# Graph network kernel: node blocks ordered by edge count, and a relational layer's block work placed at fixed steps of its edge loop

## The reference, cut to what matters

```python
def _rgcn_layer(x, src, dst, edge_type, edge_attr, W, root, bias, nn_w, nn_b):
    edge_w = edge_attr @ nn_w.T + nn_b            # (E, 256) from 32 attributes
    msg = relu(x[src] * edge_w)
    out = x @ root + bias
    for r in range(3):                            # relations
        mask = edge_type == r
        s = segment_sum(where(mask, msg, 0), dst)
        cnt = segment_sum(mask, dst)
        out = out + (s / max(cnt, 1)) @ W[r]
    return out
...
h = x
for l in range(3): h = _rgcn_layer(h, ...)
x = layernorm(x + h)
```

## Time and profile before

| what | value |
|---|---|
| time, median of 3 runs | 4121.45 us (4115.07 to 4121.66) |
| span of the profiled execution | 4117.9 us (the page gives no other time for it) |
| busy: PE, DVE, ACT, POOL | 3104.7, 2876.4, 1533.8, 2706.7 us |
| instructions | 112272 |
| granted TensorE clock, mean | 0.894 |

### The profile page before, as it was taken

The page is one execution under the profiler, slowest core; times in us unless marked ns, Lnnn a source line. Parts: engine busy times, 40 slices in busy tenths (PEclk is TensorE's granted clock), DMA queues, the critical chain, the costliest instruction groups (busy, mean ns, idle before and its releaser), DMA issues.

```text
span 4117.9 us, 112272 instructions
## 1 busy us (share of the span) xinstructions
PE 3104.7 (75%) x28301; PEld 2331.3 (57%) x28301; DVE 2876.4 (70%) x10466; ACT 1533.8 (37%) x4045; POOL 2706.7 (66%) x2886
## 2 busy tenths in 40 slices
PE   6886027777776987777648888897888888888887
PEld 4443015555554565555436666676666667666666
DVE  9998026777776677777667777766777766777777
ACT  1000006777764267777623333212333321333320
POOL 5777747777774377777647777636777745777760
PEclk8777558999998999999969999899999989999988
DMA  3222157888884578888834444314443323444430
GB/s 77 55 57 48 27 162 218 237 237 236 237 230 84 162 228 238 237 237 236 200 108 124 123 120 120 108 58 125 122 120 115 114 73 90 122 119 117 116 105 32
DMA packets 386267, 574.01 MB, mean 139 GB/s; under 512 B 134783, under 2 KB 272433, under 8 KB 386163
## 3 DMA queue, kind: packets, MB, share of 16 engines
q0 software_dynamic: 155264, 442.19, 37.8%
q1 hardware_dynamic: 176106, 123.76, 10.1%
q10 hardware_dynamic: 54794, 6.81, 1.1%
HBM read 531.37 MB, written 41.08 MB: 139 GB/s over the span
## 4 chain that ended last, share of the span: by engine, by line
PE 19%; issue 19%; DVE 16%; DVEq 10%; DMA 10%; POOL 7%; ACT 2%; ACTq 1%; POOLq 0%; SPq 0%
DMA ht<-kv_rows,gidx 6%; PE bank L1210 6%; DVE region L1873 6%; DVEq L728 4%; PE bank L1049 3%; POOL ht L584 3%; PE bank L1197 3%; DVE rings L1854 3%; DMA gring<-kv_rows,gidx 2%; DVE rings L1860 2%; POOL gring L618 2%; PE bank L1124 2%; POOL gring L584 2%; PE bank L1145 2%; PE bank L1157 1%
## 5 line engine op out<-in xcount | busy, mean ns | idle before, releaser
L618 POOL DMA_INDIRECT gring<-h_rows,gidx x1248 | 1201.1, 962 | 464.3 <-issue 317.2
L1210 PE MATMUL bank<-rings 128*128 128x96 f32 x6168 | 914.8, 297 | 247.2 <-DVE region L1873 245.3
L1210 PEld LDWEIGHTS bank<-rings 128*128 128x128 f32 x6168 | 811.0, 205 | 444.8 <-DVE region L1873 406.8
L1281 ACT ACTIVATE rings<-rings 128x512 f32<-128x512 f32 x771 | 485.6, 630 | 1366.2 <-DVE rings L1854 1313.0
L1854 DVE TENSOR_TENSOR rings<-bank,gring 128x256 f32<-128x256 f32 x1542 | 582.4, 420 | 390.1 <-PE bank L1210 195.2
L584 POOL DMA_INDIRECT gring<-kv_rows,gidx x512 | 485.7, 949 | 245.9 <-issue 133.4
L1873 DVE TENSOR_TENSOR region<-region,bank 128x192 f32 x1542 | 540.0, 350 | 131.8 <-PE bank L1210 14.7
L584 POOL DMA_INDIRECT ht<-kv_rows,gidx x512 | 486.2, 950 | 173.7 <-issue 118.4
L1322 ACT ACTIVATE ht<-ht,ntop 128x129 f32<-128x129 f32 x1024 | 413.8, 404 | 287.0 <-DVE ntop L1788 278.4
L1197 PE MATMUL bank<-nnwt,rings 64*128 64x256 f32 x3084 | 491.0, 442 | 39.1 <-DMA rings<-edge_attr_T 39.1
L559 POOL DMA_INDIRECT edge_records<-rings x416 | 408.3, 981 | 151.3 <-issue 148.5
(11 more groups left out here) (257 smaller groups left out, 4095.4 us busy)
## 6 DMA issues: line engine op xcount, KB each, us to landing
rings<-node_in_window_T SPq DMA_DIRECT2D x256, 128.0 KB
rings<-edge_attr_T SPq DMA_DIRECT2D x1548, 16.0 KB
gring<-h_rows,gidx POOLq DMA_INDIRECT x1248
kv_rows<-rows SPq DMA_DIRECT2D x50, 258.0 KB, 2.5
rows<-h_rows SPq DMA_DIRECT2D x75, 128.0 KB
gring<-kv_rows,gidx POOLq DMA_INDIRECT x512
ht<-kv_rows,gidx POOLq DMA_INDIRECT x512
region<-edge_records SPq DMA_DIRECT2D x13, 576.0 KB, 7.0
```

Of the source, the lines that this page charges most:

```text
L618: g.indirect_dma_start(out=gring_r[:, 2 * u + k, :], out_offset=None, in_=h_d[l], in_offset=bass.IndirectOffsetOnAxis(ap=gidx_r[:, half, 2 ...
L1210: ins = pe.matmul(b[:, (2 * k + c) * SEG:(2 * k + c + 1) * SEG], prod[:, slot % RL, (2 * k + c) * P:(2 * k + c + 1) * P], one, start=True, ...
L1281: act.activation(prod[:, slot % RL, :], prod[:, slot % RL, :], ACT.Relu).then_inc(s_msg, 1)
```

## The change

1. **Order of the blocks.** Before the sort, the 25 blocks are ranked by their number of edges, smallest first, the short last block always last. DVE does it in some ten small instructions between the scan of the counts and `run_tot` (three of them over 25 x 25 elements); `orders()`, some 25 more, runs after the second trip of the ranking. Blocks are then placed in that order, so that a bound holds: block number k of the order (here called by its place) is complete once a known number of pairs is done (`pairs_of_blocks`). `order_t` tells at run time which rows of the matrix the block at place k is.
2. **Steps.** The edge loop has periods of `PERIOD` = 32 steps (8 of them, plus an end of up to 32 steps) in place of 8, and three blocks start in each, at steps 4, 15 and 25. PE's eight periods are all written out; on the other engines the first period and the end are written out and the rest is a hardware loop of 32 steps. Jobs are 515 in place of 513, so 258 pairs.
3. **Block work inside the loop.** Relative to its start, each block has its own rows loaded (-11), transposed (-7), copied (-6), multiplied by `root` with the bias added by a third product (-4), kept (-3), multiplied by `W` (0, 1, 2, one relation at a step), divided and added by DVE (2, 4, 5), cleared in `racc` by ACT (6), and its rows stored by SP (14). In layer 2, DVE does the residual, the copy back and the statistics at 6 to 10, with one register loaded from `order_t` in three of these five. Blocks at places 23 and 24 start at steps 260 and 271, after the last pair (step 257).
4. DVE's bias addition (L1587), POOL's clearing and the phase after the loop are gone. A mask (`& LANDMASK`, `& FREEMASK`) is added to two register values.

```diff
-JOBS = NW + E // P
+JOBS = NWP + E // P
+PERIOD = 4 * U
+PERIODS = RPAIRS // PERIOD
+STARTS = ((4, -1), (15, 0), (25, 1))
+AFTER = 4
...
+def run_periods(eng, step, end, written=1):
+    for per in range(written):
+        for v in range(PERIOD):
+            step(per, v)
+    if written < PERIODS:
+        with eng.Fori(written, PERIODS) as per:
+            for v in range(PERIOD):
+                step(per, v)
+    for v in range(end):
+        step(PERIODS, v)
...
-        U_LOAD, U_TURN, U_TAKE, U_ROOT, U_KEEP = 0, 2, 4, 5, 7
+        AT_LOAD, AT_TURN, AT_TAKE, AT_ROOT, AT_KEEP, AT_CLEAR, AT_REST, AT_STORE = -11, -7, -6, -4, -3, 6, 6, 14
+        AT_OUT = (2, 4, 5)
...
+            step(v.tensor_reduce(sizes[:, :], by_block(cnt_w), AX.X, ALU.add))
+            after()
+            step(v.scalar_tensor_tensor(keyed[:, :], sizes[:, :], float(KEYED), iota_seg[:, 0:NT], ALU.mult, ALU.add))
+            after()
+            step(v.memset(keyed[:, NT - 1:NT], LASTKEY))
+            after()
+            step(v.tensor_tensor(earlier, across(keyed[:, :]), along(keyed[:, :]), ALU.is_lt))
+            after()
+            moved(cend, sizes)
...
+                for rel in range(NREL):                                    # PE
+                    block = block_at(per, v, rel)
+                    if block:
+                        k = block[0]
+                        n = l * NT + k
+                        if rel == 0:
+                            pe.wait_ge(s_racc, 2 * (at + min(start_of(k) - AFTER, RPAIRS)))
+                        if rel == 1:
+                            pe.wait_ge(s_root, n + 1)
+                        o = (bank[6][:, D:2 * D], bank[7][:, 0:D], bank[7][:, D:2 * D])[rel]
+                        for c in range(2):
+                            ins = pe.matmul(o, racc[:, c * NREL + rel, k * P:(k + 1) * P], wts[:, l % 2, rel, c, :],
+                                            start=c == 0, stop=c == 1)
+                        ins.then_inc(s_dn, 1)
...
+            def keep(k, slot, turn, rel):                                  # DVE
+                n = l * NT + k
+                o = orow[:, slot, :]
+                if rel == 0:
+                    v.wait_ge(s_root, n + 1)
+                    if l < 2:
+                        wait_freed(v, s_ho[l][slot], 16 * turn)
+                else:
+                    v.wait_ge(s_dv, STEPD * n + rel)
+                v.wait_ge(s_dn, NREL * n + (NREL if rel else 1))
+                product = (bank[6][:, D:2 * D], bank[7][:, 0:D], bank[7][:, D:2 * D])[rel]
+                v.scalar_tensor_tensor(o, product, inv_t[:, rel, bass.ds(k, 1)], o if rel else rootrow, ALU.mult, ALU.add)\
+                    .then_inc(s_dv, 1)
+            def rest(k, slot, i):                                          # DVE, layer 2
+                ...
+                if i in (0, 1, 4):
+                    v.reg_load([row_reg], order_t[:, bass.ds(k, 1)])
+                    row = v.snap(row_reg, min_val=0, max_val=(NT - 1) * P)
+                    own = x1_flat[:, bass.ds(row * (D // P), D)]
+                if i == 0:
+                    ins = v.tensor_tensor(o, o, own, ALU.add)
+                elif i == 1:
+                    ins = v.tensor_copy(own, o)
+                elif i == 2:
+                    ins = v.bn_stats(st_cur, o)
+                elif i == 3:
+                    ins = v.bn_aggr(mv_cur, st_cur)
+                else:
+                    ins = v.tensor_copy(ln2_mv[...], mv_cur)
+                ins.then_inc(s_fin, 1)
```

More of the change, by code:

```diff
@@ L124, in run_steps, with pair_of, alive, block_at @@
         step(trips, u)
[L127 to L138, removed]
+def run_periods(eng, step, end, written=1):
[8 more added lines that the diff above has]
+        step(PERIODS, v)
+def pair_of(per, v, lag):
+    i = v - lag
+    return per * PERIOD + i, i % U, per * (PERIOD // U) + i // U
+def alive(per, v, lag):
+    return not isinstance(per, int) or 0 <= per * PERIOD + v - lag < RPAIRS
+def block_at(per, v, offset):
+    m, at = divmod(v - offset, PERIOD)
+    for slot, (start, first) in enumerate(STARTS):
+        if at == start:
+            k = (per + m) * 3 + first
+            return None if isinstance(per, int) and not 0 <= k < NT else (k, slot, per + m - (first < 0))
+    return None
+def pairs_of_blocks(k):
+    edges = E if k == NT - 1 else E * (k + 1) // (NT - 1)
+    return -(-(edges // P + WPT * (k + 1)) // 2)
+def start_of(k):
+    return (k + 1) // 3 * PERIOD + STARTS[(k + 1) % 3][0]
 def tile_of(trip, u, lag):
@@ L183, in wait_freed @@
         eng.wait_ge(sem, value)
+assert all(pairs_of_blocks(k) <= min(start_of(k) - AFTER, RPAIRS) for k in range(NT)) and E * KEYED < LASTKEY
 def build(nc, a, out):
@@ L488, in build @@
         s_root = sem("s_root")
-        s_ho = [[sem(f"s_ho{l}_{i}") for i in range(4)] for l in range(2)]
+        s_ho = [[sem(f"s_ho{l}_{i}") for i in range(3)] for l in range(2)]
+        s_fin = sem("s_fin")
         s_ln = sem("s_ln")
@@ L870, in sync_program @@
                 else:
[L871 to L872 removed]
+                    stored(sp, l)
                 if l == 0:
@@ L1193, in step @@
                     wait_freed(pe, s_prod, at + p - 2)
-                    for pair in range(2 if live(trip, u + 1, 0, RPAIRS) else 1):
+                    for pair in range(2 if alive(per, v + 1, 0) else 1):
                         for k in range(2):
@@ L1621, in tables_of_tiles @@
-            v.wait_ge(event("tend_c"), 1)
-            step(v.tensor_copy(col_c[:, 0:3], bank[5][0:NW, 0:3 * P:P]))
-            step(v.memset(pad_c[:, 1:2], 1.0))
-            after()
-            step(v.scalar_tensor_tensor(je_c, col_c[:, 1:2], 1.0, part_f[0:NW, :], ALU.add, ALU.add))
-            step(v.tensor_copy(pad_c[:, 0:1], col_c[:, 2:3]))
+            tell("tend", v.memset(cnt_t[:, NW:NWP], 0.0))
+            v.wait_ge(event("tend_c"), 1)
+            step(v.tensor_copy(col_c[:, 0:4], bank[5][0:NWP, 0:4 * P:P]))
@@ L1874, in step @@
                             .then_inc(s_racc, 1)
-            run_steps(v, REXTRA + LAG_RACC, step, RTRIPS)
+                for rel in range(NREL):
+                    block = block_at(per, u, AT_OUT[rel])
+                    if block:
+                        keep(*block, rel)
+                for i in range(FIN if l == 2 else 0):
+                    block = block_at(per, u, AT_REST + i)
+                    if block:
+                        rest(block[0], block[1], i)
+            run_periods(v, step, PERIOD)
         block = ctx.enter_context(nc.Block())
```

407 lines of the change are left out of this document (244 added, 163 removed).

## The result

The changed kernel takes 4389.57 us (median of 4 runs, 4383.49 to 4402.01), the kernel before 4119.31 (4115.07 to 4121.66). The ratio is 1.0662, 95% interval 1.0644 to 1.068. The forecast was 4155, with a range that ended at 4235. "Slower" was right as the likeliest case, but the size was not: +270 us in place of +34.

What follows compares the result with a forecast made beforehand. The prediction took DVE, engine and queue together, to bound the edge loops. Its terms, 4 - 180 + 117 + 58 - 29 + 11 + 30 + 22, gave +33 us on 4121.45, so 4155 us, with 4066 to 4235 for 8 in 10.

Steps and rivals of the forecast that it cites:

- Slower: Whole kernel: chance 0.57 in all, of which 0.32 for the forecast case, slower by 10 to 70 us.
- What bounds the kernel: Edge loops: DVE, engine and queue together, has no free time, so whatever it gets there is paid in full.
- The ranking: Before the sort: ranking the blocks on DVE makes POOL's scatter chain begin and end later, +4 us (3 to 6).
- The boundaries: Between layers and at the end: only places 23 and 24 remain after the last pair, -180 us (-166 to -186).
- The PE term: Edge loops: PE keeps up on average, with some late edge weights and low clock; +30 us, from below 0 to +150.
- The mask: DVE's queue before each pair: with one more pair a layer, +11 us (+6 to +40), lower if fused.
- Code and branches: DVE's loop: fewer branches, -29 us; fetches at 18 returns of the longer body, +22, half of up to 45.
- keep: Edge loops on DVE: three instructions a block, 1.7 us a block for 69 blocks, +117 us (+83 to +159).
- rest: Layer 2 on DVE: residual, copies, statistics and register loads, 2.5 us a block for 23 blocks, +58 us (+30 to +80).
- the loop return is a fetch: Rival, DVE's loop: every return of the long body stalls; 4178 us at 2.5 each, 4223 at 5; chance 0.11.
- PE becomes the bound: Rival, edge loops: at the low clock PE sets the pace, +150 us in place of +30, 4275 us; chance 0.08.
- The block work hides better: Rival, DVE's queue runs ahead, so `keep` costs 1.2 us a block and `rest` 1.3; 4046 us; chance 0.33.

Runs made afterwards that it cites:

- e6_land_per_layer: e5_later_written with one landing semaphore for each layer, so the addition of l * 208 goes from VectorE's queue; 4015.3 us (0.9745 of the kernel before).
- e7r_keep_twice: e6_land_per_layer with the first `keep` of each block issued a second time into unused columns; 4029.3 us, +15.6.
- e3_all_later: The changed kernel with load, transposition, copy, root product and `keep` each two steps later; 4204.4 us (1.0222 of the kernel before).
- b1_mask_alone: The kernel before with nothing but the two masks on register values added; 4202.9 us (1.0216).
- e6r_control: e6_land_per_layer unchanged, run again beside the `keep` and `rest` experiments; 4013.7 us.
- e5_later_written: e3_all_later with VectorE's relational loop also written out; 4052.4 us (0.9839 of the kernel before).
- b5r_before_written: b1_mask_alone with VectorE's relational loop written out; 4127.5 us (1.0024 of the kernel before).
- e4_dve_written: The changed kernel with only VectorE's relational loop written out; 4240.6 us (1.0305 of the kernel before).
- e9r: e6_land_per_layer with one row-number load a block in `rest` and the sum written straight to x1, without the copy; 3992.5 us (0.9693).

## Why the prediction was wrong

*What bounds the kernel* was right: VectorE with its queue sets the pace, as long as TensorE's order does not break it. e6_land_per_layer, 37 us for one instruction of the queue, is the cleanest sign of it. "Whatever it gets there is paid in full" was too strong: in e7r_keep_twice one of three places is nearly free.

*The ranking* was right: the first scatter starts at 35.4 us, before 31.6, +3.8 for the forecast +4. *The boundaries* were right: -181 for -180. TensorE, ACT and SP are ready in time for places 23 and 24.

*The PE term is the step that failed.* The prediction took "+30 in all" from throughput: products of 2.67 us a block spread over the pairs, and the low clock. It never went through the two waits that the change gives TensorE, `wait_freed(pe, s_dv, STEPD * (n - 1) + 1)` and `wait_freed(pe, s_dv, STEPD * n)`, with their steps. Blocks start 10 or 11 steps apart. The next block's residual, 4 ahead of its start, is at step 6 or 7 of the present one; VectorE's last `keep` is at step 5. On paper that is one or two steps of slack, but TensorE is steps ahead of VectorE, as it must be to have weights and sums ready; the slack is negative. The same holds for the transposition (step 3 or 4) and the first `keep` (step 2). The loss is 185 us (e3_all_later) against 30. The closing list named a sign, waits of VectorE for the sums (L1210) and the edge weights above 100 us, but it could not tell: the row for L1210 was 195.2 us already before the change, by the register loads. The row that tells is that of the additions, 14.7 before and 114.5 after, and it means TensorE's order, not its rate.

*The mask* was mis-sized: +6 to +40 with the pair, the low end taken on the guess that it would be fused. The high end was added up wrongly too: by the prediction's own 0.09 us for a separate instruction it is 774 x 0.09 + 5 = 75, not 40. The mask breaks a fusion that existed, and costs 86 us (b1_mask_alone). The row L737 FUSED_REGOPS was there to read in the trace before.

*Code and branches*: the mechanism was named, at half price. All 18 returns stall, 3.1 us each, so +56 for +22. With the 29 us of branches saved the two terms are +27, forecast -7.

*`keep`* was put at +117. Its measured price depends on the form of the loop. In e6r_control, where the block's place and the wait values are constants, layer 1's loop is 574.5 us for 258 pairs; pairs without block work run at 2.01, 1.57, 2.01 and 2.95, 8.54 for four, so 258 / 4 x 8.54 = 551 and 24 us a layer are left, some 71 in all or 0.34 for each of the 207 inside the loops. In e3_all_later these values are still computed from the loop register, as in the change as made. There the same four pairs take 2.09, 1.71, 2.09 and 3.24 (medians), 9.13 together, so that of 644.0 us pairs take 589 and six returns 19, and 36 a layer are left, some 110 in all. That is an upper figure, as other waits are in it; but for the form that was predicted the term was about right.

*`rest`*: layer 2's loop is 50 us longer than layer 1's in both kernels (forecast +58). The load of one register was put at 0.16 and takes 0.31 us. These loads read tables in on-chip memory, and the three measured ones (0.31 for 1 register, 0.60 for 8, 1.35 for 20) don't lie on the straight line that the prediction drew through two of them:

```profile
L2013 DVEq TENSOR_LOAD <-order_t x75: 300/311/323, 3660.4 to 4370.3; - x75
```

The account with measured terms, `keep` at 71: +4 - 181 + 71 + 50 + 27 + 86 + 5 (one more pair a layer) + 185 = +247, of +270. With `keep` at 110 it is +286, so the two figures hold +270 between them. A second account needs no price of an instruction. The change in equal form is -75 (e5_later_written against b5r_before_written), the masks are +86, TensorE's two waits +185, and VectorE's loop costs 149 us in the changed kernel (returns and arithmetic, e4_dve_written) where the same edit was worth 75 in the kernel before with the masks (b1_mask_alone less b5r_before_written), +74: together +270. That these parts add was tested by e5_later_written, to 3 us. The prediction had only the returns of this last term as a term of its own, and had the arithmetic inside `keep` and `rest`.

Of the rivals, "the loop return is a fetch" was true and too small. "PE becomes the bound" had the right engine and the wrong mechanism; e3_all_later refutes a bound. "The block work hides better" asks for `keep` at 83 or less: that came true in the written-out form (71) and is not shown for the form as made.

## What to carry to other kernels

When work is put at fixed steps of a pipelined loop, write beside each wait the step at which the other engine signals and add how many steps the waiting engine runs ahead; a wait on an engine that is normally behind must be later than that lead, or everything queued behind it stands as well. Here two steps were worth 185 us. Where an engine's queue sets the pace, count the queue's instructions as closely as the engine's, and see in the trace whether a new one breaks a fused one. Judge a restructuring only after its side costs are taken away: this one was 6.6% slower as made, 1.8% faster in equal form, and 3.1% faster than the kernel before with the repairs and two savings of its own (e6, e9r).

## What the hardware showed that was not expected

A return of VectorE's loop is free (0.22 to 0.26 us) up to a body of 276 recorded instructions and costs 2.7 to 3.5 us from 384 to 647, almost whatever the length. Masking a register value that was copied and added to in one FUSED_REGOPS (0.044 us) gives a MOVE and two ALU_OPs, and 0.15 us more a pair.

TensorE's granted clock was lower where the engine waited more. In layer 1's edge loop it was 0.87 of full speed in the changed kernel and 0.97 in e6r_control, with the same products and a loop that was 137 us shorter; without the two waits alone (e3_all_later) it was 0.93. The windows of e6r_control:

```profile
2762.00:3336.00 574.00, 511.05 (x3535) 419.19 (x3532) 434.71 (x1222) 190.05 (x327) 396.51 (x432) 0.97 0.43 120
```

The two waits are not the only cause of a lower clock: b1_mask_alone has neither, and its layer 1 has 0.90 where the kernel before has 0.92. For the part of the time at the lower of the two levels, 1.2 GHz, the work behind a stall is slower too. How much of the 185 us came that way was not separated.
